# A graph network on one core: gathered tiles counted, handed over and given back in groups of four instead of eight

## What is computed

```python
edge_index = jnp.stack([src, dst])
h = jnp.maximum(_layernorm(x, axis=-1), 0.0)
x = x + _L0_gnn_ref(h, edge_index, L0_gnn_W1, L0_gnn_b1, L0_gnn_W2, L0_gnn_b2)
h = jnp.maximum(_layernorm(x, axis=-1), 0.0)
x = x + _L1_gnn_ref(h, L1_gnn_W, L1_gnn_b, src, dst)
h = jnp.maximum(_layernorm(x, axis=-1), 0.0)
x = x + _L2_gnn_ref(h, edge_index, edge_weight, L2_gnn_W, L2_gnn_b)
h = jnp.maximum(_layernorm(x, axis=-1), 0.0)
x = x + _L3_gnn_ref(h, node_vec1, src, dst, L3_gnn_Wf, ...)
```

## Time and profile before

| | us |
|---|---|
| median of 3 runs | 13334.67 |
| the runs | 13330.79, 13342.0, 13334.67 |
| the profiled execution | 13330.65 |
| its span, first to last instruction | 13328.8 |
| POOL busy | 8446.9 (63%) |
| PE busy | 6231.2 (47%) |
| DVE busy | 3324.7 (25%) |
| ACT busy | 1199.0 (9%) |

### The profile page before, as it was taken

One profiled execution on the slowest core, in us unless ns is written; L12 is line 12 of the kernel. 1 busy time (PEld: TensorE's weight loads), 2 busy tenths in 40 slices (PEclk: granted clock), 3 DMA queues, 4 the chain that ended last, 5 costly groups with the idle time before them and its releaser, 6 DMA issues. The chain is left out here.

```text
span 13328.8 us, 104959 instructions
## 1 busy us (share of the span) xinstructions
PE 6231.2 (47%) x28873; PEld 5495.9 (41%) x28873; DVE 3324.7 (25%) x11523; ACT 1199.0 (9%) x2452; POOL 8446.9 (63%) x8914
## 2 busy tenths in 40 slices
PE   1666666833333343333334333333455555555666
PEld 1666666722232332222233232223354444444555
DVE  3111111111111131111113211212232222223777
ACT  2000000100000010000001000000010000000776
POOL 5666666466666666666665666666655555555776
PEclk5555555655555565555556555555676666666887
DMA  3111111111111111111111111111134444444332
GB/s 88 45 46 46 46 46 45 41 48 46 46 46 47 46 49 48 47 46 46 46 46 44 50 46 46 46 46 46 41 104 127 124 130 130 127 132 128 119 117 99
DMA packets 600384, 905.24 MB, mean 68 GB/s; under 512 B 150231, under 2 KB 443087, under 8 KB 573215
## 3 DMA queue, kind: packets, MB, share of 16 engines
q0 software_dynamic: 254048, 522.40, 15.8%
q10 hardware_dynamic: 247712, 225.10, 5.2%
q1 hardware_dynamic: 98111, 151.31, 3.5%
HBM read 749.71 MB, written 150.14 MB: 68 GB/s over the span
## 5 line engine op out<-in xcount | busy, mean ns | idle before, releaser
L412 POOL DMA_INDIRECT rows_buf<-table,tile_cols x6252 | 5961.1, 953 | 3069.5 <-issue 1835.5
L542 PE MATMUL psum<-rows_buf,onehot 128*128 x13312 | 3678.6, 395 | 4757.0 <-issue 4517.1
L542 PEld LDWEIGHTS psum<-rows_buf,onehot 128*128 128x128 f32 x13312 | 2906.7, 283 | 5175.6 <-issue 5170.7
L489 DVE TENSOR_SCALAR onehot<-iota_col,dl_tab 128x128 f32<-128x128 f32 x4992 | 1018.9, 294 | 5757.6 <-PE psum L542 2314.3
L412 POOL DMA_INDIRECT rows_buf<-ptable,tile_cols x1563 | 1489.6, 953 | 1036.4 <-SPq L432 567.3
L1337 PE MATMUL psum<-rows_buf 128*128 128x131 f32 x3328 | 942.4, 376 | 1192.9 <-issue 665.5
L1337 PEld LDWEIGHTS psum<-rows_buf 128*128 128x128 f32 x3328 | 692.0, 258 | 1344.5 <-issue 749.7
L544 PEld LDWEIGHTS psum<-ew_tab,onehot 128*128 128x128 f32 x3328 | 914.9, 328 | 388.1 <-issue 387.9
L1324 DVE SCALAR_TENSOR_TENSOR rows_buf<-rows_buf,sc,psum 128x130 f32<-128x130 f32 x1664 | 555.7, 348 | 1789.4 <-remote 1027.0
L544 PE MATMUL psum<-ew_tab,onehot 128*128 128x1 f32 x3328 | 705.5, 274 | 397.8 <-issue 395.9
L489 DVE TENSOR_SCALAR onehot<-iota_col,dl_tab,ew_tab 128x128 f32<-128x128 f32 x1664 | 435.6, 359 | 1810.3 <-PE psum L542 995.5
(11 more groups left out here) (274 smaller groups left out, 2710.1 us busy)
## 6 DMA issues: line engine op xcount, KB each, us to landing
work<-dl_rows ACTq DMA_DIRECT2D x104, 1024.0 KB
zrows<-rows_buf ACTq DMA_DIRECT2D x104, 1024.0 KB
work<-zrows SPq DMA_DIRECT2D x104, 1024.0 KB, 4.9
rows_buf<-table,tile_cols POOLq DMA_INDIRECT x6252
rows_buf<-ptable,tile_cols POOLq DMA_INDIRECT x1563
table<-acc SPq DMA_DIRECT2D x42, 448.0 KB, 3.0
ptable<-rows_buf SPq DMA_DIRECT2D x14, 455.0 KB, 4.1
table<-work SPq DMA_DIRECT2D x14, 448.0 KB, 3.0
```

Source lines behind the costliest of these rows:

```text
L412: pool.indirect_dma_start(out=slots[:, t % (groups * GT), 0:width], out_offset=None, in_=tab, in_offset=bass.IndirectOffsetOnAxis(ap=idx_t ...
L489: last = nc.vector.tensor_scalar(onehot[:, q % 2 * HALF + u, :], iota_col[:], dl_tab[:, col:col + 1], ew_tab[:, col:col + 1] if weighted e ...
L542: last = nc.tensor.matmul(held, m, rows_t, start=False, stop=False, skip_group_check=True)
```

## The change

`GT` goes from 8 to 4, and every number that counts groups doubles, so that the sizes in tiles stay: a ring of 64 slots (z stage 32), 32 tiles of lead (z stage 16). There are 392 groups of tiles where there were 196, the last of them empty, so `tiles_of` is bounded at zero. `gathered` becomes sixteen semaphores instead of eight. To make room for them, `rows_free` becomes one semaphore that counts on through all five stages (`freed` is the count that earlier stages left), and the last stage waits on the z stage's two store semaphores, counted on by `stored`, instead of two of its own. Lines after line 404 move down by one. The core of the diff:

```diff
-GT = 8
-SLOTS = 4 * GT
+GT = 4
+SLOTS = 8 * GT
 READY_STEP = 4
-RGROUPS = 8
-LEAD = 4
-Z_RGROUPS = 4
-Z_LEAD = 2
+RGROUPS = 16
+LEAD = 8
+Z_RGROUPS = 8
+Z_LEAD = 4
...
-    assert TGROUPS == -(-NT // GT) and 2 * SLOTS * ACW >= RSLOTS * F
+    assert 2 * SLOTS * ACW >= RSLOTS * F
...
-        s_free = [sem(f"rows_free{no}") for no in range(PASSES)]
+        s_free = sem("rows_free")
...
-            return min(GT, NT - g * GT)
+            return max(0, min(GT, NT - g * GT))
...
         def gather_tiles(pool, no, tab, slots, groups, width):
 
+            freed = no * (TGROUPS - RGROUPS)
             for g in range(TGROUPS):
                 if g >= groups:
-                    pool.wait_ge(s_free[no], g - groups + 1)
+                    pool.wait_ge(s_free, freed + g - groups + 1)
...
-                    sp.sem_inc(s_free[no], 1)
+                    sp.sem_inc(s_free, 1)
...
-        s_z = [sem(f"msg_z{h}") for h in range(2)]
+        s_z, stored = s_zout, 16 * (HALVES // 2)
...
-                    dve.wait_ge(s_z[q % 2], 16 * (q // 2 + 1))
+                    dve.wait_ge(s_z[q % 2], stored + 16 * (q // 2 + 1))
```

## The result

| | before | after |
|---|---|---|
| median of 4 runs each, us | 13332.73 | 13258.38 |
| the profiled execution, us | 13330.65 | 13266.87 |
| pass 0, first to last gather | 2266.7 | 2265.9 |
| pass 1 | 2229.2 | 2230.3 |
| pass 2 | 2228.8 | 2228.0 |

The ratio after to before is 0.994, with a 95% interval from 0.9925 to 0.9955: 74 us faster. The forecast was 201 us faster. The sign and the range (12900 to 13350) held, the size did not.

What follows compares the result with a forecast made beforehand. Bound: a per-tile price of gathering (1.427 us), plus, in z, DVE's walk to the release item. Terms -180 (z), -20 (pass 0), -2 (z start), +1 (setup) sum to -201: 13334.7 to 13134 us; range 12900 to 13350.

Steps and rivals of the forecast that it cites:

- The passes: Releases in passes 1 to 3: hardly a walk to shorten, 0 taken, between 86 us won and 10 us lost.
- a price per gathered tile: Passes 1 to 3: each gathered tile costs 1.427 us however waits are cut; POOL issues at 1.25 and pays back waiting.
- Pass 0: Pass 0, two products an item, lasts 38 us longer; if that is walk, half goes: 20 us won, 0 to 38.
- Releases in z: z stage: groups of four shorten DVE's walk to the release item; 180 us won, 122 to 208.
- My lower end: z releases: mean walk 4.5 to 2.5 items, cycles perhaps 14 tiles instead of 16; 122 us won.
- POOL goes on 1 to 2 us after DVE's run begins: Sign in z's timeline: POOL resumes 1 to 2 us after DVE's run begins, not 3.4.
- Waits in z of 390 us in 120 to 190 pieces: Sign on the gathers' line: z near 2327 us, with waits of about 390 us in 120 to 190 pieces.
- Start of z and setup: DVE begins z after 4 landed tiles, 2 us won (0 to 5); larger release table, 1 us lost (0 to 2).
- Counting: 944 more POOL waits and doubled SP counts of landings and releases: 0 on the path.
- nothing is won: Rival, 16%: POOL resumes earlier but its gathers slow PE and DVE earlier; z keeps 1.605 us a tile, 13335 us.
- The passes gain too: Rival, 12%: the per-tile price is not real and waits of all stages shrink; put at 12800 us.
- Slower: Rival, 14%: sooner restarts cut runs before z's PE clock rises; 143 us slower, 13478 us.

Runs made afterwards that it cites:

- release_alone: Changed kernel with landings handed over in groups of eight as before, only giving back in groups of four, in all five stages: 13235.41 us, ratio 0.9929.
- z_no_gram_2: Changed kernel with z's second product of each item left out and a unit of two in z: 11596.36 us where the kernel before takes 11606.
- z_no_store_8: Changed kernel with a sixteenth of z's store, unit eight in z, wide products and units 16, 8, 2 in passes 1 to 3: 11601.98 us, before 11606.
- z_no_store_2: Changed kernel with a sixteenth of z's store, unit two in z, passes 1 to 3 only 32, 32, 16 tiles ahead: 12539.69 us, before 11606.

## Why the prediction was right or wrong

- **The passes** (0, between -86 and +10): right. They moved by +1.1, -0.8 and +1.0 us. The reason given, a price per gathered tile that no cutting changes, is borne out by units from 2 to 16 and by half the gathers taking half the time. The second reason, that at 0.46 us "there is hardly a walk to shorten", is not: the mean walk is 0.60 to 0.96 us, by where PE's run is taken to begin (idle time of no more than 0.3 or 0.5 us in it), and walks of 2 us and more cost the passes nothing either.
- **Pass 0** (-20, 0 to -38): the best value failed, the end at 0 held. It moved by -0.8. The step that failed was "if that is walk": it is the second product's share in the price, 30 us where pass 2 was given one.
- **Releases in z** (-180, 122 to 208): the mechanism was right and the term mis-sized. It is -95 us, outside even the range I gave it. Two steps failed. First, I took both cycles of the earlier trace rows for the stage: their walks of 3.35 and 3.42 us are above its mean of 2.42. Second, "six items of walk become two" in the same number of cycles: the mean walk went from 4.6 items to 2.9, and the cycles became shorter and more, 125 in place of 102. My lower end had this mechanism (4.5 items to 2.5, shorter cycles). It had 14 tiles a cycle and took what was idle as 278 us; with the measured walk of 1.27 us over 12.4 tiles, 0.102 us a tile or 159 us a stage, against walks of 247 us, the same working gives 88 of the 95 us that came. The value nearer to the upper end was the choice that cost most.
- **POOL goes on 1 to 2 us after DVE's run begins**: right, 1.27 us in the mean. Waits in z of 390 us in 120 to 190 pieces: 459.4 in 129; the count was right, the sum was not. Waits of the passes were 285 us where 265 to 280 was said, with no effect on their length.
- **Start of z and setup** (-2 and +1): the first gather of pass 0 came 0.5 us later (248.6 against 248.1). The z stage's earlier start can't be seen beside pauses between the stages that differ by 13 us from one execution to the next.
- **Counting** (0): right. release_alone has the finer waits without the finer landings and is no slower; the 944 waits more cost POOL nothing on the path.
- **The sum**: -201 against -64 in the profiled executions and -74 in the medians. 85 us of the difference are the z term, 19 pass 0, and the rest is the pauses between the stages, which I had taken for constant.
- **Rivals**: "nothing is won" had the counter-effect right in kind: a sooner POOL does end the run sooner, and the stops went from 102 to 125. "The passes gain too" fell with the flat passes. "Slower" fell: the granted clock over z is 0.66 after and 0.64 before.

## What to carry to other kernels

A wait that ends at the next multiple of a batch costs the walk to it once in every cycle; when the batch is halved the walk halves, but the cycles shorten too, so multiply by the new number of cycles, and take the mean walk over the stage and not that of the cycles that one happened to look at. A stage with a price per transfer hardly answers to the size of a batch, as long as the batch is well under half of the ring; several stages with different cuttings and equal length show it before any experiment. Split release and hand-over before changing both: here one brought everything, and in units of two where it pays (z) it brings twice what the change did.

## What the hardware showed beside

- **The price per gather is not a constant of the chip.** On the third group's chip the kernel before took 11606 us, and the passes of z_no_gram_2, which are those of the changed kernel (what was expected of it stands below), ran at POOL's own pace: 1957.9 us in pass 1, 1.254 a gather, with POOL hardly waiting. PE there works through the items of each group of landed rows and then waits for the next (its timeline: start, duration, idle before and its ender):

```profile
3001.64 3.78 PE L552 MATMUL psum<-rows_buf,onehot 128*128 x16 [6.12 <-SPq L427]
3011.90 3.78 PE L552 MATMUL psum<-rows_buf,onehot 128*128 x16 [6.48 <-SPq L427]
3016.87 3.61 PE L552 MATMUL psum<-rows_buf,onehot 128*128 x16 [1.19 <-SPq L427]
```

  There are none of the single matmuls with idle time put down to "issue" of the earlier trace rows. There is no walk to shorten then: in that group z took 1961.4 us at a unit of eight (z_no_store_8) and 1963.8 at two (z_no_store_2), without one stop of over 1.3 us. The changed kernel itself was not run there; it should bring nothing. The records give the third and the fourth group the same chip number with 11606 and 13230 us for the same kernel, so what differs need not be the chip itself.


> As the run before, with a unit of two in z and the passes as in the changed kernel. Theory, pace of PE's items: z comes to 2260 to 2290 us, half of the 115 us that stay above 2229 at a unit of two. Rival, another floor: z stays at 2330 to 2350.

- **What holds PE up while gathers are issued is not the fetch of its instructions by DMA.** From the start of one run of PE's matmuls to the start of the next it works off about the same number of instructions in pass 0 and in pass 1 (medians of 171 and 168 in the trace of before; a run is 16 matmuls or more with no more than 0.3 us idle between two), though an item has ten in the one and five in the other; the starts are 23 and 45 us apart, 16 gathers there and 32 here. That looks like a supply of instructions. The Trainium skill, page "Runtime: NRT & Kernel Launch", section on instruction fetch mechanics, says that engines refill their instructions in blocks by DMA and that this is mostly hidden. The trace of before agrees. Pass 1 has these DMA queues (queue, kind: packets, MB, share of 16 engines):

```profile
q0 software_dynamic: 49967, 102.46, 18.1%
q8 instruction: 33, 0.54, 0.1%
```

  Each packet of q8 has 16384 bytes and takes 0.88 to 1.50 us. There are 33 for PE's 8488 instructions of pass 1, 64 for its 16437 of pass 0 and 60 for its 15212 of z, one per some 256, so they are PE's. Of the 1373 us that PE stands idle for over 0.7 us at a time in pass 1, they overlap 9 us, and most of the slow phases between two runs of matmuls hold none of them (43 of 54). In pass 1 of z_no_gram_2 there are 33 of them as well, as long as here, and PE has no slow phase. So something else slows PE while POOL issues gathers; no run isolates it, and it stays open.
